# Low parts of five expert weight halves made on GpSimd instead of VectorE

## The reference

```python
shared = new_gelu(xf @ Wfc_s + bfc_s) @ Wproj_s + bproj_s
probs = softmax(xf @ Wr); topk_p, topk_i = top_k(probs, 2)      # 8 experts
for e in range(8):
    h = new_gelu(xf @ Wfc[e] + bfc[e]) @ Wproj[e] + bproj[e]
    routed = routed + h * gate[:, e:e + 1]
out = x + shared + routed
```

## Time and profile before

| what | value |
|---|---|
| median of 3 runs | 845.7 us (844.99 to 848.27) |
| the profiled execution | 847.65 us, its span 845.9 us |
| PE busy | 769.6 us (91% of the span) |
| DVE busy | 627.3 us (74%) |
| ACT busy | 365.7 us (43%) |
| POOL busy | 228.6 us (27%) |
| mean granted clock of TensorE | 0.971 of full speed |

### The profile page before, as it was taken

One profiled execution on the slowest core, in us unless ns is written; L12 is line 12 of the kernel. 1 busy time (PEld: TensorE's weight loads), 2 busy tenths in 40 slices (PEclk: granted clock), 3 DMA queues, 4 the chain that ended last, 5 costly groups with the idle time before them and its releaser, 6 DMA issues.

```text
span 845.9 us, 21759 instructions
## 1 busy us (share of the span) xinstructions
PE 769.6 (91%) x6791; PEld 628.9 (74%) x6791; DVE 627.3 (74%) x1988; ACT 365.7 (43%) x833; POOL 228.6 (27%) x221
## 2 busy tenths in 40 slices
PE   3989898989865999999999999999999999989995
PEld 1666666766643878888888888888888887667673
DVE  4578888889766998888887666666666666666664
ACT  4545454544423444455553333333333334444442
POOL 2210101011011003566621333333333333223232
PEclk9899999999966999999999999999999999999998
DMA  5465676665323446788873444445544443344431
GB/s 182 143 162 140 185 137 179 144 176 104 70 51 106 133 144 206 226 236 243 242 217 61 68 65 65 65 65 65 65 67 67 67 64 57 57 57 63 67 64 27
DMA packets 163123, 97.28 MB, mean 115 GB/s; under 512 B 105260, under 2 KB 158408, under 8 KB 163016
## 3 DMA queue, kind: packets, MB, share of 16 engines
q1 hardware_dynamic: 149720, 78.81, 39.0%
q0 software_dynamic: 13296, 17.09, 12.0%
HBM read 38.73 MB, written 36.15 MB: 89 GB/s over the span
## 4 chain that ended last, share of the span: by engine, by line
PE 51%; issue 25%; DVE 10%; DMA 10%; ACT 2%; POOL 1%; SPq 1%; POOLq 0%; ACTq 0%; DVEq 0%
PE bank_kv L1270 7%; PE bank_kv L1271 7%; PE bank_kv L1272 7%; PE bank_st L1247 5%; DMA expert_buffers<-rows_by_expert 5%; PE bank_st L1249 4%; PE bank_st L1248 4%; PE bank L1247 4%; PE bank L1249 4%; PE bank L1248 4%; PE bank_kv L1263 3%; DMA stage_w<-in_L_ffn_Wproj 2%; DVE w_parts L1034 2%; DVE expert_buffers L1047 2%; PE bank_kv L1264 1%
## 5 line engine op out<-in xcount | busy, mean ns | idle before, releaser
L1270 PE MATMUL bank_kv<-w_parts,expert_buffers 128*128 (+1 forms) x656 | 179.0, 273 | 5.0 <-DVE expert_buffers L1048 4.7
L733 ACT ACTIVATE expert_buffers<-bank_st,bias_columns 128x256 f32<-128x256 f32 (+1 forms) x248 | 108.1, 437 | 166.3 <-PE bank_st L1249 119.2
L1272 PE MATMUL bank_kv<-w_parts,expert_buffers 128*128 (+1 forms) x656 | 178.8, 273 | 0.0
L1271 PE MATMUL bank_kv<-w_parts,expert_buffers 128*128 (+1 forms) x656 | 178.8, 273 | 0.0
L733 ACT ACTIVATE expert_buffers<-bank,bias_columns 128x256 f32<-128x256 f32 (+1 forms) x248 | 108.2, 436 | 142.2 <-PE bank L1249 76.6
L1047 DVE TENSOR_SCALAR expert_buffers<-expert_buffers 128x256 f16<-128x256 f32 x328 | 101.7, 310 | 78.1 <-ACT expert_buffers L733 76.9
L1048 DVE SCALAR_TENSOR_TENSOR expert_buffers<-expert_buffers 128x256 f16<-128x256 f32 x328 | 139.4, 425 | 11.3
L594 POOL DMA_INDIRECT out<-expert_buffers,token x71 | 118.8, 1673 | 15.6 <-issue 15.6
L1247 PE MATMUL bank_st<-expert_buffers,w_parts 128*128 128x256 f16 (+1 forms) x368 | 88.3, 249 | 11.3 <-DMA expert_buffers<-rows_by_expert 7.5
L575 POOL DMA_INDIRECT rows_by_expert<-rows,dest_rows x64 | 66.5, 1039 | 99.0 <-ACT expert_buffers L733 91.0
L1249 PE MATMUL bank_st<-expert_buffers,w_parts 128*128 128x256 f16 (+1 forms) x368 | 88.4, 249 | 0.0
(11 more groups left out here) (189 smaller groups left out, 1555.9 us busy)
## 6 DMA issues: line engine op xcount, KB each, us to landing
rows_by_expert<-w_parts SPq DMA_DIRECT2D x12, 795.0 KB, 5.8
stage_w<-in_L_ffn_Wfc SPq DMA_DIRECT2D x16, 512.0 KB, 4.1
stage_w<-in_L_ffn_Wproj SPq DMA_DIRECT2D x16, 512.0 KB
expert_buffers<-in_L_ffn_bproj SPq DMA_DIRECT2D x46, 128.0 KB
rows<-in_x SPq DMA_DIRECT2D x16, 256.0 KB, 3.3
x_residual<-rows SPq DMA_DIRECT2D x16, 256.0 KB, 4.7
expert_buffers<-x_residual SPq DMA_DIRECT2D x16, 256.0 KB, 3.3
out<-expert_buffers SPq DMA_DIRECT2D x16, 256.0 KB, 4.1
```

Source lines behind the costliest of these rows:

```text
L733: act.activation(spare[:, at], hid[c % 4][:, 0:width(G)], ACT.Gelu_apprx_tanh, bias=bias, scale=UNSCALE).then_inc(s["gelu_done"], 1)
L1270: pe.matmul(y, g[:, 0, tile(t)], w_hi, start=f == 0 and t == 0, stop=False, skip_group_check=True)
L1271: pe.matmul(y, g[:, 0, tile(t)], w_lo, start=False, stop=False, skip_group_check=True)
L1272: op = pe.matmul(y, g[:, 1, tile(t)], w_hi, start=False, stop=f == FC - 1, skip_group_check=True)
```

## The change

For the first five up halves (`POOL_HALVES` = 5, shared blocks 0 to 4) ACT, after making the high part, also scales the staging buffer in place, and only then signals `w1_hi`. DVE leaves out both `split_last` pieces of the up half in these blocks. POOL runs `convert_lo` for these halves, before its wait for `routed`.

```diff
+    POOL_HALVES = 5
@@ gpsimd @@
             pool.wait_ge(s["route_iota"], 5)
+            for half in range(POOL_HALVES):
+                convert_lo(half, HALVES - 2 * E + half)
             pool.wait_ge(s["routed"], 1)
@@ scalar, convert_last @@
                 act.wait_ge(s[loaded], (HALVES - 2 * E + half + 1) * 16)
-                act.activation(w[:, half * 2048:half * 2048 + 1024], stage, ACT.Copy, scale=W_SCALE).then_inc(s[done], 1)
+                op = act.activation(w[:, half * 2048:half * 2048 + 1024], stage, ACT.Copy, scale=W_SCALE)
+                if w is w1 and half < POOL_HALVES:
+                    op = act.activation(stage, stage, ACT.Copy, scale=W_SCALE)
+                op.then_inc(s[done], 1)
@@ vector, body @@
                     if isinstance(G, int) and G < NSH:
-                        if f in (4, 5):
+                        if f in (4, 5) and G >= POOL_HALVES:
                             split_last(G, w1, stage1[:, :], "w1_hi", "w1_lo", f - 4)
```

## The result

The changed kernel takes 857.29 us (median, 855.71 to 858.59), the kernel before 846.99 us on the same chip: ratio 1.0123, interval 1.0095 to 1.0151, 10.3 us more. Slower had been forecast, but by 6.1 us and at 851.8 us: 857.3 lies above the range of 848.5 to 854.3. Of the 5.5 us between the forecast and the result, 1.3 us are the base: with a fourth run the median of the kernel before is 846.99 instead of 845.7 us. The other 4.2 us are the change's own.

A forecast was written before the change was run, and what follows sets the result against it. VectorE's load was taken to bound shared blocks 1 to 4. Block 0 losing 2.1 us and blocks 1 to 4 losing 8.9 instead of 4.94 (4.0 more) gave 845.7 + 6.1 = 851.8 us, range 848.5 to 854.3.

The forecast's parts named there:

- What bounds the stage: Shared blocks 1 to 4: VectorE, busy nearly without a gap, makes TensorE wait and lose 4.94 us together.
- ScalarE's copy costs nothing: Blocks 0 to 4: the in-place copy delays the Gelu of chunk 3 by 0.95 us, but VectorE isn't there yet.
- GpSimd's subtraction stops DVE to its end: Blocks 0 to 4: one VectorE instruction moves nothing until GpSimd's 2.14 us subtraction ends; TensorE stands 2.10 us at chunk 3.
- T + 2.44: Forecast start of GpSimd's subtraction in block 1: 2.44 us after the Gelu of chunk 2 starts.
- The cost of the hold: Blocks 0 to 4: VectorE stopped by GpSimd costs 2.1 us in block 0 and 4.0 in blocks 1 to 4.
- the sum: Whole kernel: 2.1 us in block 0 plus 4.0 net in blocks 1 to 4, 6.1 us more, 851.8 us.
- the clock falls: Rival: TensorE's stalls lower its clock; one block at half speed would cost 10 us, 861 us; chance 0.04.
- not held up: Rival: in the shared blocks VectorE and GpSimd run side by side, gaining 3.8 us, 841.9 us; chance 0.08.
- Partly hidden: Rival: part of the hold falls into VectorE's idle time, near 3 us less lost in all, 848.7 us; chance 0.10.
- The spared pieces: Two VectorE pieces removed per block free 1.20 us, more than the 0.8 us backlog, so chunk 2 starts at once.

The follow-up runs named there:

- no_subtraction: Changed kernel without GpSimd's subtraction, ScalarE's second copy writing the low half itself; blocks 0 to 4 took 53.56 us, whole ratio 0.9963 to the kernel before.
- in_place_only: Kernel before plus only ScalarE's in-place scaling copy, low parts still made by VectorE; blocks 0 to 4 took 56.45 us, whole ratio 1.0008.
- filled_stall: Changed kernel with 16 matmuls into an unused PSUM bank before down(3) in blocks 1 to 4; blocks 0 to 4 took 62.31 us, whole ratio 1.0101.
- later_subtraction: Changed kernel with GpSimd's subtraction started only when chunk 4 of the block is split; blocks 0 to 4 took 60.16 us, whole ratio 1.0052.
- hold_added: Kernel before plus a ScalarE copy and a GpSimd subtraction on unused regions in blocks 0 to 4; those took 66.71 us, whole ratio 1.0119.
- vector_delay: no_subtraction plus about 2.2 us of VectorE work in unused regions before chunk 3 of blocks 0 to 4; those took 67.15 us, whole ratio 1.0120.
- the filled kernels: filled_stall and its repeat beside the changed kernel on one chip; blocks 0 to 4 took 62.31 and 62.30 us, whole ratios 1.0101 and 1.0095.
- routing_spread: Kernel before with the twenty routing parts spread over blocks 0 to 6 and scatters over 7 to 14; blocks 0 to 4 53.71 us, whole ratio 1.0017.
- half_subtraction: Changed kernel with GpSimd subtracting only 512 columns and VectorE the other 512 in chunk 5; blocks 0 to 4 took 57.55 us, whole ratio 1.0012.

## Why the prediction was wrong, point by point

- *What bounds the stage*: right. DVE's load makes blocks 1 to 4 long; spared of two pieces in each of five blocks it gives 2.83 us back (no_subtraction).
- *ScalarE's copy costs nothing*: right, +0.06 us (in_place_only).
- *GpSimd's subtraction stops DVE to its end*: right, in moment (T + 2.44), length (2.13 us) and place in blocks 1, 3 and 4 (the residual addition, in block 1 held for 1.71 us beyond its 0.69); in block 2 it was the high part of chunk 3. The longest stalls came out as 1.94, 1.84, 1.95 and 1.95 us in blocks 1 to 4 where 2.10 was written, and 1.77 in block 0.
- *The cost of the hold*: the forecast of 6.1 us is confirmed where the clock is kept up: 5.92 us (filled_stall, in the stretch). Its parts came out near the sum's: 1.8 us instead of 2.1 in block 0, 4.1 instead of 4.0 in blocks 1 to 4.
- *The clock*: this is the step that failed. The prediction put "the clock falls" among the rivals at 0.04, because PE would still be busy for over 80% of a block and because stalls of 1 us had left the clock at 1.00, and it left the term out of the sum. The rows it went by had no stall of PE over 1.0 us in this stage, so they could not exclude it. The trace of the kernel before does hold a fall, in the first stage, where PE has less to do:

```profile
236.24 0.23 PE L1140 MATMUL bank<-w_parts 1*128 1x77 f16 x2 [1.69 <-DVE w_parts L881]
...
234.50:237.35 2.85, 1.10 (x18) 0.75 (x16) 2.46 (x13) 0.59 (x4) 1.32 (x1) 1.00 0.10 35
237.35:240.77 3.42, 1.07 (x5) 0.72 (x5) 2.56 (x11) 2.19 (x7) 0.00 (x0) 0.50 0.19 38
```

The clock went from 1.00 to 0.50 1.1 us after a wait of 1.69 us had ended. That was a reason for more than 0.04.

In the changed kernel the clock fell behind three of the four stalls of 1.8 to 1.95 us in blocks 1 to 4, and cost 66.85 - 62.31 = 4.54 us. The price was also mis-sized: not 10 us for a whole block at half speed (with which the sum would be 861.8, not 861), but 1.4 to 1.7 us each, 16 matmuls at half speed. 5.92 + 4.54 = 10.46 us in the stretch, and the medians differ by 10.3. That the whole time falls by as much when the clock is kept up is not shown: with the fillers it fell by 0.8 us.
- *The other rivals*: "not held up" is excluded by the rows of 2.40 and 2.22 us. "Partly hidden" did not occur in the change, but later_subtraction shows what it is worth: +3.8 us, near the 3 us priced.
- *The spared pieces*: the sum starts each block with DVE free of its backlog, and the hold then sets the time of chunk 3. hold_added, which keeps the backlog, shows what that freedom is worth beside the hold: nothing in blocks 1, 2 and 4, 1.26 us in block 3, where a late DVE had the evacuation still ahead of it. The sum does not say this, and needs it in block 3.

What stays open: why the clock falls behind some of these stalls and not behind others (in the changed kernel behind 1.94 and 1.95 us, not behind 1.84; in hold_added behind 1.97 and 2.96, not behind 1.83 and 1.95; in vector_delay behind 2.4 and 2.8 us, not behind 2.1 and 2.2), and the 4 us between what the filled kernels gain in the stretch and in the whole.

## What to carry to other kernels

Before work goes from VectorE to GpSimd, look for a place in the trace where the two already run side by side and read the longer duration of VectorE's instruction there: in this kernel VectorE lost up to the whole length of GpSimd's instruction (2.1 us) for the 1.2 us that it was spared. Then ask what VectorE still has to do, behind the hold, before the instruction that TensorE waits for. What it was spared counts only if it changes that; it did in one of four blocks. If the work must move, short pieces, or a moment at which VectorE is ahead, cost a half or less of the same work in one piece ahead of the critical instruction (5.1 and 3.8 us instead of 10.5 in the stretch). And when a change makes TensorE stand for near 2 us in a stage that had only stalls of 1 us, put a fall of its clock into the sum: a few matmuls into an unused bank will show whether it is that.

## What was not expected of the hardware

- TensorE's granted clock fell to 1.2 GHz 0.2 to 0.8 us after it had resumed from waits of 1.94 and 1.95 us, in blocks in which PE was busy for 86% of the time (12.32 of 14.26 us in block 1). It did not after 1.77 and 1.84 us (blocks 0 and 2), nor after 1.95 us in hold_added (block 4), nor after 2.1 and 2.2 us in vector_delay, nor after 2.47 us in the routed stage of routing_spread (at 442.5), nor in blocks 0 to 4 after waits of up to 1.0 us (half_subtraction, later_subtraction). It fell without GpSimd too.
- When the two engines meet, the one that comes second waits, in both directions: GpSimd's 2.13 us became 2.62 when it came 0.05 us after a VectorE instruction, VectorE's 0.28 us became 2.22. An instruction of VectorE that reads PSUM and one SBUF operand ran beside GpSimd undisturbed, also when it came second (L1031 of hold_added, two in 0.76 us at 283.56, GpSimd from 283.37). One that reads only a single SBUF operand did not: L1053, the 0.28 us that became 2.22.
- Even a routing instruction of 8 columns (0.17 us) took 0.63 us beside a piece of GpSimd's.
